# A two-layer graph network: layer 1's edge loop built on 128-wide one-hots and node-major sums, node blocks worked outside the loops

## The chip, the cores and the metric

One core of one Trainium2 chip runs the whole program in one launch. The metric is device time in microseconds. Below, PE is TensorE, DVE is VectorE, ACT is ScalarE, POOL is GpSimd and SP is SyncE.

## What is computed

There are 6250 nodes with 128 features and 200000 edges, sorted by their target `dst`; all numbers are float32. The reference, cut down:

```python
h = relu(layernorm(x))
z = (h @ W).reshape(N, 8, 16)                      # 8 heads of 16
el, er = (z * attn_l).sum(-1), (z * attn_r).sum(-1)
e = leaky_relu(el[src] + er[dst], 0.2)
a = exp(e - segment_max(e, dst)[dst])
agg = segment_sum(z[src] * a, dst) / segment_sum(a, dst)
x = x + agg + bias                                 # layer 1
h = relu(layernorm(x)); s, v = h @ W_up_s, h @ W_up_v      # 32 scalars, 32 vectors of 3
w0, w1, w2, w3 = split(silu(silu(ef @ A1 + b1) @ A2 + b2) @ A3)
msg = [s*y0*w0, (v.y)*w3, s*y*w1, v*y0*w2]         # per edge, s and v of src
x = x + segment_sum(msg, dst) / 10 @ W_out         # layer 2
```

## The kernel before

Both layers walk over the edges in 196 groups of 1024 (`NG`, `GE`): 8 edges (`T`) for each of the 128 partitions. A loop body of four groups (`U`) is run 49 times. The rows that the edges need are gathered from a table in HBM (`z_tab` of 136 columns in layer 1, `up_tab` of 128 in layer 2) by POOL: one indirect DMA takes 128 rows, so a group costs eight of them (L401), and a layer 1568. Four slots of `rows` let POOL run ahead; it waits for the group's indices (a small DMA that SP issues) and for `rows_free`, which DVE raises once it has read a slot.

Since the edges are sorted, a group's targets lie in a window of 48 nodes (`WIN`). **Layer 1** for a group: DVE compares the targets with a row of 0 to 47 and so makes the one-hot `hot` (L743, 384 elements in each partition); PE turns it (L977), ACT copies it out, and PE multiplies it with 48 rows of `er` that SP fetched (L987), which gives each edge its target's value. DVE computes scores (L799 to L804), ACT takes the exponential (L488), DVE multiplies the rows (L809, two halves of 512 elements). PE then sums with the *messages* as the stationary operand and `hot` as the moving one, 48 columns wide (L1004), once more for the denominators (L1006), and DVE adds the result to 48 columns of `acc_a` and `den_acc` (L771, L773), which hold features in the partitions and nodes along the free axis. **Layer 2** has an edge network on PE and ACT (L1040 to L1050, L502, L504), products on DVE (L872 to L890) and sums on PE (L1083, L1085) in the same form, added at L860 and L862.

A block of 128 nodes is finished inside the loops, as soon as no later edge can reach it (a table `ready` says when). In layer 1 that is `stage_sums` on ACT, `turn_sums` on PE and `divide_block` on DVE (L753 to L763), which also takes the block's statistics for the next norm. In layer 2 it is `stage_block`, `map_block` (four matmuls with the output weights, L1062), `add_block` (L843) and a store. After a loop only the last one to three blocks are left.

Ahead of layer 1 come loads, POOL's fills (L393 to L397), the targets' conversion (L564), statistics of x in seven chunks (L546), and `node_lin` with `node_rows`, which make `z_tab`; SP stores it in seven transfers. Between the layers the accumulators are filled with zero by POOL (L422 to L424), while ACT, PE and DVE make `up_tab` (L447, L453, L929, L934, L621, L629). POOL starts layer 2's gathers once that table is stored. The order on every engine is that of the code, and nothing reorders it.

## Time and profile before

| | |
|---|---|
| time, median of 3 runs | 4219.83 us (4218.35 to 4221.5) |
| span of the profiled execution | 5708.3 us |
| first gather, last of layer 1, first and last of layer 2 (start) | 91.58, 2845.44, 2942.36, 5666.08 us |
| PE busy in that span | 3872.9 us |
| POOL busy | 3121.2 us |
| DVE busy | 1850.8 us |
| ACT busy | 547.9 us |

Of the profiled execution there is no time but its span, and the span is far longer than the runs that were timed. A row of the timeline gives the start, how long the work took, and in brackets how long the engine had stood idle and what ended that. "128*128 128x48 x2" at a matmul is the stationary tile, then the moving one; one float32 matmul of the program leaves two records. Rows of POOL are the making of an indirect DMA's descriptors, not the transfer. A row of windows gives the stretch, its length, busy us (and instructions) of PE, PE's weight loads, DVE, ACT and POOL, then the granted clock of PE as a share of full speed, the DMA engines' share and GB/s.

### The profile page before, as it was taken

The page shows a single profiled execution, that of the slowest core. Times are in us where ns is not written, and L with a number is a line of the kernel's source. Part 1 is how long each engine was busy: PE and PEld are TensorE (multiplying, and loading weights), DVE is VectorE, ACT ScalarE, POOL GpSimd, SP SyncE. Part 2 cuts the span into 40 slices and gives each one's busy share as a digit, 9 for nine tenths or more (in the row PEclk, how much of TensorE's full clock was granted, in tenths as well). Part 3 has the DMA queues.
Part 4 walks back from the last instruction along what each step waited for, and adds up shares of the span by engine and source line. Part 5 has one row for each costly group of instructions (what it writes and reads, how often), then busy time and mean ns, then how long its engine had stood idle before and what let it go on. Part 6 is the DMA issues. An engine that isn't in the chain of part 4 may idle for free.

```text
span 5708.3 us, 68375 instructions
## 1 busy us (share of the span) xinstructions
PE 3872.9 (68%) x18070; PEld 2962.4 (52%) x18071; DVE 1850.8 (32%) x4774; ACT 547.9 (10%) x1093; POOL 3121.2 (55%) x3153
## 2 busy tenths in 40 slices
PE   3566666766666666666657776776777776667767
PEld 2455555555555555555545555555555555555545
DVE  6122222222222222222234443433333434333334
ACT  1000000000000000000021111111111111111111
POOL 4555555555555555555535555555555555555554
PEclk8555555555555555555567777777777877777777
DMA  3111111111111111111111111111111111111111
GB/s 75 40 40 40 40 40 41 41 42 40 41 40 41 40 41 39 41 40 40 40 43 41 42 45 41 44 45 41 42 43 43 44 44 41 44 40 43 42 41 34
DMA packets 259081, 239.77 MB, mean 42 GB/s; under 512 B 179890, under 2 KB 205596, under 8 KB 259068
## 3 DMA queue, kind: packets, MB, share of 16 engines
q0 software_dynamic: 100352, 212.14, 15.2%
q1 hardware_dynamic: 158572, 26.68, 2.6%
q10 hardware_dynamic: 144, 0.80, 0.0%
q14 instruction: 9, 0.07, 0.0%
q8 instruction: 4, 0.07, 0.0%
HBM read 229.11 MB, written 10.23 MB: 42 GB/s over the span
## 4 chain that ended last, share of the span: by engine, by line
another core or an unknown queue 43%; PE 22%; issue 17%; DVE 11%; DVEq 4%; ACT 2%; DMA 0%; ACTq 0%; SPq 0%
PE pair L1085 5%; PE pair L1050 5%; DVE share L809 4%; PE pair L1044 3%; PE pair L1083 3%; PE pair L1040 2%; DVEq L768 2%; ACT share L502 1%; PE pair L1062 1%; PE pair L1004 1%; PE pair L987 1%; DVE share L743 1%; DVE share L800 1%; DVE share L799 1%
## 5 line engine op out<-in xcount | busy, mean ns | idle before, releaser
L401 POOL DMA_INDIRECT rows<-z_tab,idx x1568 | 1531.6, 977 | 1290.3 <-DVEq L813 748.9
L401 POOL DMA_INDIRECT rows<-up_tab,idx x1568 | 1549.4, 988 | 1208.6 <-DVEq L896 718.1
L1004 PE MATMUL pair<-share 128*128 128x48 f32 x3136 | 1000.7, 416 | 122.6 <-issue 122.3
L1004 PEld LDWEIGHTS pair<-share 128*128 128x128 f32 x3136 | 808.4, 317 | 279.4 <-issue 273.3
L1085 PE MATMUL pair<-share 128*128 128x144 f32 x3136 | 859.4, 359 | 129.8 <-issue 129.3
L1083 PEld LDWEIGHTS pair<-share 128*128 128x128 f32 x3136 | 587.2, 219 | 443.2 <-issue 342.9
L1050 PE MATMUL pair<-a_bd,share 128*128 128x256 f32 x1576 | 465.9, 448 | 394.1 <-ACT share L504 371.1
L877 DVE TENSOR_TENSOR share<-share,y_sb 128x768 f32<-128x768 f32 x392 | 375.6, 958 | 977.1 <-remote 662.1
L1083 PE MATMUL pair<-share 128*128 128x48 f32 x3136 | 585.7, 269 | 140.0 <-issue 121.2
L1085 PEld LDWEIGHTS pair<-share 128*128 128x128 f32 x3136 | 561.3, 221 | 128.6 <-issue 128.0
L987 PE MATMUL pair<-er_win,share 96*128 96x32 f32 x1576 | 377.2, 404 | 333.0 <-issue 268.4
L1050 PEld LDWEIGHTS pair<-a_bd,share 128*128 128x128 f32 x1576 | 341.7, 227 | 460.2 <-ACT share L504 381.8
L1006 PE MATMUL pair<-share 128*8 128x48 f32 x3136 | 521.0, 264 | 74.5 <-issue 73.7
L987 PEld LDWEIGHTS pair<-er_win,share 96*128 96x128 f32 x1576 | 351.2, 328 | 370.0 <-issue 368.8
L977 PE MATMUL pair<-ident,share 128*96 128x128 f32 x788 | 214.6, 428 | 367.4 <-DVE share L743 359.5
L887 DVE TENSOR_TENSOR share<-rows,pair 128x384 f32<-128x384 f32 x784 | 396.6, 548 | 10.0 <-DMA rows<-up_tab,idx 10.0
L799 DVE TENSOR_TENSOR share<-rows,pair 128x64 f32<-128x64 f32 x196 | 43.3, 221 | 1067.9 <-remote 681.7
L1044 PE MATMUL pair<-share,a_bd 128*128 128x512 f32 x396 | 283.9, 808 | 137.3 <-ACT share L502 133.6
L977 PEld LDWEIGHTS pair<-ident,share 128*96 128x96 f32 x788 | 126.5, 188 | 413.7 <-DVE share L743 386.0
L1006 PEld LDWEIGHTS pair<-share 128*8 128x8 f32 x3136 | 164.1, 91 | 242.9 <-issue 103.6
L502 ACT ACTIVATE share<-pair,vec 128x512 f32<-128x512 f32 x198 | 136.0, 687 | 1368.3 <-remote 737.8
L809 DVE TENSOR_TENSOR share<-rows,share 128x512 f32<-128x512 f32 x392 | 251.9, 683 | 0.0
(138 smaller groups left out, 2085.3 us busy)
## 6 DMA issues: line engine op xcount, KB each, us to landing
rows<-z_tab,idx POOLq DMA_INDIRECT x1568
rows<-up_tab,idx POOLq DMA_INDIRECT x1568
idx<-in_src SPq DMA_DIRECT2D x396, 4.0 KB
er_win<-er_tab SPq DMA_DIRECT2D x396, 3.0 KB
ef_sb<-in_edge_f SPq DMA_DIRECT2D x198, 32.0 KB
z_tab<-rows SPq DMA_DIRECT2D x7, 476.0 KB, 3.1
y_sb<-in_edge_y SPq DMA_DIRECT2D x198, 16.0 KB
x_sb<-in_x SPq DMA_DIRECT2D x7, 448.0 KB, 6.9
```

The source lines that it names most:

```text
L401: pool.indirect_dma_start(out=rows[:, s, t, 0:width], out_offset=None, in_=table, in_offset=bass.IndirectOffsetOnAxis(ap=indices[:, t:t + ...
L809: ins = v.tensor_tensor(msg[:, h, ts, :].rearrange("p t (h f) -> p t h f", f=PER_HEAD), rows[:, s, ts, 0:HIDDEN].rearrange("p t (h f) -> p ...
L877: v.tensor_tensor(wy[:, hf, :, :].rearrange("p t (k w) -> p t k w", k=4), bc(eq[:, hf, :, :], 2, 4), bc(y_sb[:, s, ts, :], 3, WIN), ALU.mult)
L887: v.tensor_tensor(prod[:, hf, :, half, 0:96].rearrange("p t (i u) -> p t i u", u=MUL), g_v, bc(tp[:, :, lo:lo + 32], 2, 3), ALU.mult)
L977: mm = t.transpose(bank[0][0:2 * WIN, j * P:(j + 1) * P], hot[:, s, 2 * j:2 * j + 2, :].rearrange("p t w -> p (t w)"), ident[:, :])
L987: mm = t.matmul(bank[6 + h][:, j * 32:j * 32 + 32], hotT[0:2 * WIN, h, j * P:(j + 1) * P], er_win[0:2 * WIN, s, :], start=True, stop=True)
L1004: t.matmul(bank[2 + h][:, 0:WIN], msg[:, h, i, :], hot[:, s, i, :], start=(i == 0), stop=(i == T - 1))
L1006: mm = t.matmul(bank[4 + h][0:HEADS, 0:WIN], a_sb[:, h, i, :], hot[:, s, i, :], start=(i == 0), stop=(i == T - 1))
L1044: t.matmul(bank[5], a2_bd[:, :], h1_sb, start=True, stop=True).then_inc(s_l2["h2"], 1)
L1050: mm = t.matmul(bank[2 * h + j // 2][:, (j % 2) * 256:(j % 2) * 256 + 256], h2_sb[:, h, j * P:(j + 1) * P], a3_bd[:, :], start=True, stop= ...
L1083: t.matmul(bank[6 + h][:, 0:WIN], prod[:, hf, j, 0, :], wy[:, hf, j, 0:WIN], start=st, stop=en, skip_group_check=True)
L1085: mm = t.matmul(bank[6 + h][:, WIN:4 * WIN], prod[:, hf, j, 1, :], wy[:, hf, j, WIN:4 * WIN], start=False, stop=en, skip_group_check=True)
```

## The change

Layer 1's loop is written anew, with a layout of its own over the accumulators (`lay`).

- The one-hot is 128 wide: `hot` has 1024 elements in each partition, made from `dst_col`. It is now the *stationary* operand, the messages the moving one: 136 columns, 16 features and a one for each head, so that the denominators come out of the same matmul. Sums have nodes in the partitions (`sums_all`, 98 slots of 64 nodes' step with 136 columns), and DVE adds one slot for each group.
- The turned one-hot is no longer made by PE and ACT. SP reads the group's 1024 targets into all partitions (`load_targets`), and DVE compares them with each partition's node number (`turned_hot`).
- `er` stays in SBUF (`er_slots`), together with a bound that keeps the exponent at or under zero; the score has three DVE instructions and not four.
- The indices are loaded once (`idx_all`); DVE copies eight columns for each group (`set_idx`), in layer 2 too.
- The node blocks leave both loops. Between the layers a loop of seven takes chunks of 7 blocks; at the end PE maps all 49 blocks straight from the accumulators.
- More of the targets' arithmetic stands ahead of layer 1, in `set_windows`.

The core of the diff (`divide_block`, `stage_sums`, `turn_sums`, `stage_block`, `map_block` and `add_block` are taken out):

```diff
+        SUM0 = COLS + MW
+        sums_all = lay(COLS, 1 + SLOTS1, MW)
+        sums_at = lay(SUM0, SLOTS1, MW)
+        sums_even = lay(SUM0, NB, 2, MW)
+        sums_odd = lay(COLS, NB, 2, MW)
+        AUX = SUM0 + SLOTS1 * MW
+        er_slots = lay(AUX, NB, 2, 2 * HEADS)
+        er_flat = lay(AUX, SLOTS1, 2 * HEADS)
+        dst_col = lay(AUX + 32 * NB, NG + 1, T)
+        node_id = lay(AUX + 32 * NB + (NG + 1) * T, NG + AHEAD)
+        dst_bc = lay(AUX + 32 * NB + (NG + 1) * T + NG + AHEAD, 2, GE)
...
+            def load_targets(s, group):
+                sp.dma_start(dst_bc[:, s % 2, :], dst_tab[bass.ds(group * GE, GE)].partition_broadcast(P)).then_inc(s_l1["in"][s % 2], 16)
...
-            for s_l, tab, width in ((s_l1, z_tab, ZW), (s_l2, up_tab, HIDDEN)):
-                if s_l is s_l2:
-                    pool.wait_ge(s_mid["agg_staged"], NB)
-                    pool.memset(den_acc, 0.0).then_inc(zeroed, 1)
-                    pool.memset(max_acc, 0.0).then_inc(zeroed, 1)
-                    pool.memset(acc_a[:], 0.0).then_inc(zeroed, 1)
-                    table_stored(s_mid)
...
+                            hold(pool, idx_set, (n + before) * U + (s + 1))
+                            hold(pool, freed, n * (2 * U) + (2 * s + 2))
...
+            pool.wait_ge(G["summed"], 1)
+            pool.memset(acc[:], 0.0).then_inc(zeroed, 1)
+            table_stored(s_mid)
...
+                cols = dst_col[:, 0:NG, :]
+                own.after(v.tensor_tensor(cols, dst_rel[:, :, :], bc(slot_f[:, :], 2, T), ALU.subtract))
+                turn_back = tab_sb[:, 0:BU + 4, :].rearrange("p a f -> p (a f)")[:, 0:NG * T]\
+                    .rearrange("p (g t) -> p g t", t=T)
+                own.after(v.scalar_tensor_tensor(out=turn_back, in0=cols, scalar=float(P), in1=bc(odd_f[:, :], 2, T),
+                                                 op0=ALU.is_ge, op1=ALU.mult))
+                own.after(v.tensor_tensor(cols, cols, turn_back, ALU.subtract))
+                own.after(v.tensor_tensor(dst_rel[:, :, :], dst_rel[:, :, :], bc(win_f[:, :], 2, T), ALU.subtract))
...
+            v.tensor_copy(er_slots[HALF:P, :, 1, :], er_slots[HALF:P, :, 0, :]).then_inc(G["er_ready"], 1)
+            v.tensor_copy(er_slots[0:HALF, 0:NB - 1, 1, :], er_slots[0:HALF, 1:NB, 0, :]).then_inc(G["er_ready"], 1)
+
+            def set_idx(s, group):
+                v.tensor_copy(idx[:, s, :], idx_all[:, bass.ds(group, 1), :].rearrange("p a t -> p (a t)"))\
+                    .then_inc(idx_set, 1)
...
             def one_hot(s, group):
-
                 v.tensor_tensor(hot[:, s, :, :],
-                                bc(dst_rel[:, bass.ds(group, 1), :].rearrange("p a t -> p (a t)"), 2, WIN),
-                                bc(iota[:, :], 1, T), ALU.is_equal).then_inc(s_l1["hot"], 1)
...
+                                bc(dst_col[:, bass.ds(group, 1), :].rearrange("p a t -> p (a t)"), 2, P),
+                                bc(iota[:, :], 1, T), ALU.is_equal)
...
+            def turned_hot(s, group, arrived):
+                dve.wait_ge(s_l1["in"][s % 2], arrived)
+                v.tensor_scalar(hotT[:, s % 2, :], dst_bc[:, s % 2, :], node_id[:, bass.ds(group, 1)], None,
+                                ALU.is_equal).then_inc(s_l1["turned"], 1)
...
-                        own_l1.after(v.tensor_tensor(e3[0], el_e, er_e[:, :, 0:8], ALU.add))
-                        own_l1.after(v.scalar_tensor_tensor(out=e3[1], in0=e3[0], scalar=NEG_SLOPE, in1=e3[0],
-                                                            op0=ALU.mult, op1=ALU.max))
-                        own_l1.after(v.tensor_tensor(e3[2], e3[1], er_e[:, :, 8:16], ALU.subtract))
-
-                        v.tensor_scalar(e3[3], e3[2], 0.0, None, ALU.min).then_inc(s_l1["score"], 1)
...
+                        own_l1.mark(v.tensor_tensor(e_sb[:, h, :, 0, :], el_e, er_e[:, :, 0, :], ALU.add))
+                        own_l1.after(v.scalar_tensor_tensor(out=e_sb[:, h, :, 1, :], in0=el_e, scalar=NEG_SLOPE,
+                                                            in1=er_e[:, :, 1, :], op0=ALU.mult, op1=ALU.add))
+                        v.tensor_tensor(e2_sb[:, h, :, :], e_sb[:, h, :, 0, :], e_sb[:, h, :, 1, :], ALU.max)\
+                            .then_inc(s_l1["score"], 1)
+                        set_idx(s, q * U + (s + U))
+                        turned_hot(s, q * U + (s + AHEAD), k * IN1 + q * 32 + (16 * (s // 2) + 32))
                         one_hot((s + 1) % U, q * U + (s + 1))
...
-                            ins = v.tensor_tensor(msg[:, h, ts, :].rearrange("p t (h f) -> p t h f", f=PER_HEAD),
-                                                  rows[:, s, ts, 0:HIDDEN].rearrange("p t (h f) -> p t h f", f=PER_HEAD),
-                                                  bc(a_sb[:, h, ts, :], 3, PER_HEAD), ALU.mult).then_inc(s_l1["msg"], 1)
-                        dve.wait_ge(s_l1["msg"], (n * U + (s + 1)) * 2)
-                        dve.sem_inc(s_l1["rows_free"], 1)
+                            v.scalar_tensor_tensor(
+                                out=msg[:, h, ts, :].rearrange("p t (h f) -> p t h f", f=RW),
+                                in0=bc(a_sb[:, h, ts, :], 3, RW), scalar=1.0,
+                                in1=rows[:, s, ts, 0:MW].rearrange("p t (h f) -> p t h f", f=RW),
+                                op0=ALU.min, op1=ALU.mult).then_inc(s_l1["msg"], 1)
...
+                own_sum.mark(v.tensor_tensor(even[HALF:P], even[HALF:P], odd[HALF:P], ALU.add))
+                own_sum.after(v.tensor_tensor(even[0:HALF], even[0:HALF], before[0:HALF], ALU.add), hold)
+                cells = even.rearrange("p k (h f) -> p k h f", f=RW)
+                own_sum.after(v.tensor_scalar(rden, cells[:, :, :, PER_HEAD:RW].rearrange("p k h a -> p k (h a)"), TINY,
+                                              None, ALU.max), hold)
+                own_sum.after(v.reciprocal(rden, rden), hold)
+                own_sum.after(v.tensor_tensor(part_rows.rearrange("p k (h f) -> p k h f", f=PER_HEAD),
+                                              cells[:, :, :, 0:PER_HEAD], bc(rden, 3, PER_HEAD), ALU.mult), hold)
+                own_sum.after(v.tensor_tensor(x_sb[:, bs, :], x_sb[:, bs, :], part_rows, ALU.add), hold)
+                own_sum.mark(v.memset(rden, 0.0))
+                norm_stats(q)
...
-                for j in range(HT):
-                    mm = t.matmul(bank[6 + h][:, j * 32:j * 32 + 32], hotT[0:2 * WIN, h, j * P:(j + 1) * P],
-                                  er_win[0:2 * WIN, s, :], start=True, stop=True)
+                at = pe.value_load(slot_i[0:1, bass.ds(group + 1, 1)], min_val=0, max_val=SLOTS1 - 1)
+                pe.wait_ge(s_l1["turned"], count + (AHEAD + 1))
+                for i in range(T):
+                    mm = t.matmul(bank[6 + h][:, i * 16:i * 16 + 16], hotT[:, h, i * P:(i + 1) * P],
+                                  er_flat[:, bass.ds(at, 1), :].rearrange("p a f -> p (a f)"), start=True, stop=True)
                 mm.then_inc(s_l1["er"], 1)
 
-            with pe.Fori(0, passes) as k:
-                turn(0, k * (NG + 1))
...
-                            t.matmul(bank[2 + h][:, 0:WIN], msg[:, h, i, :], hot[:, s, i, :],
-                                     start=(i == 0), stop=(i == T - 1))
-                            mm = t.matmul(bank[4 + h][0:HEADS, 0:WIN], a_sb[:, h, i, :], hot[:, s, i, :],
+                                pe.wait_ge(s_l1["msg"], n * (2 * U) + (2 * U + 2 * s + i // HT + 1))
+                            if i == 0:
+                                pe.wait_ge(s_l1["added"], n * U + (s + 1))
+                            mm = t.matmul(bank[2 + h][:, 0:MW], hot[:, s, i, :], msg[:, h, i, :],
                                           start=(i == 0), stop=(i == T - 1))
...
+            pe.wait_ge(s_l2["added"], passes * NG + 1)
+            for c in range(BI):
+                for hf, (lo, hi) in enumerate(HALVES):
+                    m = 2 * c + hf
+                    if m >= 4:
+                        pe.wait_ge(s_out["added"], m - 3)
+                    for b in range(lo, hi):
+                        nodes = slice((c * BU + b) * P, (c * BU + b) * P + P)
+                        for i in range(4):
+                            mm = t.matmul(bank[m % 4][:, (b - lo) * P:(b - lo) * P + P],
+                                          acc_a[:, nodes] if i == 0 else acc_b[:, i - 1, nodes],
+                                          wo_a[:, :] if i == 0 else wo_b[:, i - 1, :], start=(i == 0), stop=(i == 3))
+                    mm.then_inc(s_out["agg"], 1)
```

DVE in layer 1's loop, one group (`acc<-acc` are `hotT` and `hot`, which lie in `acc` now; `share` holds the scores, `a_sb` and `msg`). Before:

```order
L799 TENSOR_TENSOR share<-rows,pair 128x64
...
L800 SCALAR_TENSOR_TENSOR share<-share 128x64
...
L802 TENSOR_TENSOR share<-share,pair 128x64
...
L804 TENSOR_SCALAR share<-share 128x64
...
L743 TENSOR_TENSOR share<-dst_rel,iota 128x384
...
L809 TENSOR_TENSOR share<-rows,share 128x512 x2
...
L771 TENSOR_TENSOR acc_a<-acc_a,pair 128x48
...
L773 TENSOR_TENSOR acc_b<-acc_b,pair 8x48
```

The same place in the changed kernel:

```order
L783 TENSOR_TENSOR share<-rows,pair 128x8x8
L784 SCALAR_TENSOR_TENSOR share<-rows,pair 128x8x8
...
L786 TENSOR_TENSOR share<-share 128x64
...
L726 COPY idx<-idx_all 128x8
...
L745 TENSOR_SCALAR acc<-acc 128x1024
...
L739 TENSOR_TENSOR acc<-acc,iota 128x1024
...
L794 SCALAR_TENSOR_TENSOR share<-share,rows 128x544 x2
...
L754 TENSOR_TENSOR acc<-acc,pair 128x136
```

The copy of indices and the comparison of 1024 elements are new, the one-hot has 1024 elements for 384, and the message's two halves have 544 elements for 512 in another form of instruction.

DVE between the layers, one of seven passes of the new loop (`acc<-acc` are the sums of two slots brought together; seven BN_STATS, of which one is shown, follow, then seven BN_AGGR):

```order
L822 TENSOR_TENSOR acc<-acc 64x7x136
...
L823 TENSOR_TENSOR acc<-acc 64x7x136
...
L825 TENSOR_SCALAR share<-acc 128x56
...
L827 RECIPROCAL share<-share 128x56
...
L828 TENSOR_TENSOR share<-acc,share 128x896
...
L830 TENSOR_TENSOR x_sb<-x_sb,share 128x896
...
L831 MEMSET share 128x56
L515 BN_STATS share<-x_sb 128x6
```

None of this stood behind layer 1's loop before; there `divide_block` was left for the last blocks alone.

## Rows read from the trace of the kernel before

**Rows 1.** Top of the page, and the POOL groups of its section 5 (mean ns; idle before).
```profile
span 5708.3 us, 68375 instructions
...
L401 POOL DMA_INDIRECT rows<-z_tab,idx x1568 | 1531.6, 977 | 1290.3 <-DVEq L813 748.9
L401 POOL DMA_INDIRECT rows<-up_tab,idx x1568 | 1549.4, 988 | 1208.6 <-DVEq L896 718.1
```

**Rows 2.** Timeline of PE in layer 1: start us, duration us, work [idle before <-releaser].
```profile
1520.11 0.24 PE L1004 MATMUL pair<-share 128*128 128x48 f32 x1 [1.86 <-issue]
```

**Rows 3.** Timeline of POOL, from several stretches of the span.
```profile
91.58 1.31 POOL L401 DMA_INDIRECT rows<-z_tab,idx  x1 [67.02 <-issue]
93.19 6.76 POOL L401 DMA_INDIRECT rows<-z_tab,idx  x1 [0.30 <-issue]
...
109.01 0.94 POOL L401 DMA_INDIRECT rows<-z_tab,idx  x1 [0.30 <-issue]
...
2831.72 0.94 POOL L401 DMA_INDIRECT rows<-z_tab,idx  x1 [0.30 <-issue]
...
2845.44 0.94 POOL L401 DMA_INDIRECT rows<-z_tab,idx  x1 [0.30 <-issue]
...
2942.36 0.95 POOL L401 DMA_INDIRECT rows<-up_tab,idx  x1 [33.27 <-issue]
...
5666.08 0.94 POOL L401 DMA_INDIRECT rows<-up_tab,idx  x1 [0.30 <-issue]
```

**Rows 4.** Windows of all engines, one without gathers in layer 1, one at the start.
```profile
2855.00:2890.00 35.00, 33.62 (x159) 26.20 (x158) 10.44 (x36) 3.05 (x8) 0.00 (x0) 0.50 0.01 1
...
0.00:10.00 10.00, 0.00 (x0) 0.01 (x1) 4.55 (x5) 1.29 (x2) 9.48 (x12) 1.00 0.90 242
```

**Rows 5.** Timeline of VectorE and POOL side by side.
```profile
92.45 6.68 DVE L714 TENSOR_TENSOR x_sb<-x_sb,bias_bc 128x6272 f32<-128x6272 f32 x1
...
111.97 0.22 DVE L799 TENSOR_TENSOR share<-rows,pair 128x64 f32<-128x64 f32 x1 [4.08 <-DMA rows<-z_tab,idx]
...
1504.77 0.55 DVE L743 TENSOR_TENSOR share<-dst_rel,iota 128x384 f32<-128x384 f32 x1
...
1505.23 1.28 DVE L809 TENSOR_TENSOR share<-rows,share 128x512 f32<-128x512 f32 x2
...
1505.87 1.47 POOL L401 DMA_INDIRECT rows<-z_tab,idx  x1 [0.30 <-issue]
```

**Rows 6.** Timeline of the start: VectorE's first cast, POOL's fill, statistics of one chunk.
```profile
2.07 16.09 POOL L395 MEMSET acc_b<- 128x19200 f32 x1
...
5.71 18.65 DVE L564 CAST dst_rel<-share 128x1568 f32<-128x1568 int32 x1 [4.66 <-DMA share<-in_dst]
...
32.28 1.45 DVE L546 BATCH_NORM_STATS2 share<-x_sb 128x6 f32 x7 [0.28 <-issue]
```

**Rows 7.** Timeline between the layers.
```profile
2877.31 0.22 DVE L799 TENSOR_TENSOR share<-rows,pair 128x64 f32<-128x64 f32 x1 [3.62 <-PE pair L987]
...
2889.91 0.18 DVE L773 TENSOR_TENSOR acc_b<-acc_b,pair 8x48 f32 x1
...
2890.58 0.98 DVE L739 TENSOR_SCALAR dst_rel<-dst_rel 128x1568 f32<-128x1568 f32 x1
...
2894.87 8.85 DVE L763 COPY share<-share 128x2 f32 x1 [0.16 <-DVE share L762]
...
2909.46 0.34 ACT L447 ACTIVATE share<-share,flags 128x49 f32<-128x49 f32 x1 [15.31 <-DVEq L605]
```

**Rows 8.** Timeline of the end of layer 2.
```profile
5676.19 0.83 PE L1062 MATMUL pair<-wo_b,share 128*128 128x128 f32 x6
...
5689.26 1.01 DVE L887 TENSOR_TENSOR share<-rows,pair 128x384 f32<-128x384 f32 x2
...
5700.65 1.39 PE L1062 MATMUL pair<-wo_b,share 128*128 128x128 f32 x6
...
5705.48 0.33 SPq L385 DMA_DIRECT2D out<-x_sb  x1
```

More of the change, by code:

```diff
@@ L713, in _ @@
+            for s in range(U):
+                set_idx(s, s)
             dve.wait_ge(loads["bias"], 16)
             own.after(v.tensor_tensor(x_sb[:, :, :], x_sb[:, :, :], bc(bias_bc[:, :], 1, NB), ALU.add))
-            own.after(v.tensor_reduce(least, wide[0:1, 0:NG].rearrange("p (q s) -> p q s", s=U), AX.X, ALU.min))
-            shift = 1
-            while shift < GI:
-                own.after(v.tensor_tensor(least[:, 0:GI - shift], least[:, 0:GI - shift], least[:, shift:GI],
-                                          ALU.min))
-                shift *= 2
@@ L724, in _ @@
-            own.after(v.tensor_scalar(ends, iota[0:1, 0:NB - 1], float(P), float(P), ALU.mult, ALU.add))
-            own.after(v.tensor_tensor(past, bc(least, 2, NB - 1), bc(ends, 1, GI), ALU.is_ge))
-            own.after(v.tensor_reduce(least, past, AX.X, ALU.add))
-            v.memset(ready[:, 0:2], 0)
-            v.tensor_copy(ready[:, 2:GI + 2], least).then_inc(G["ready_set"], 1)
-            dve.wait_ge(G["ready_set"], 1)
-            dve.wait_ge(G["er_stored"], 32)
+            dve.wait_ge(G["lin_stored"], 16)
@@ L738, in next_pass @@
                 own_pass.after(v.tensor_copy(win_i[0:1, 1:NG + 1], win_f[0:1, :]))
-                own_pass.after(v.tensor_scalar(dst_rel[:, 0:NG, :], dst_rel[:, 0:NG, :], -float(WIN), None, ALU.add))
-            def one_hot(s, group):
-                v.tensor_tensor(hot[:, s, :, :],
-                                bc(dst_rel[:, bass.ds(group, 1), :].rearrange("p a t -> p (a t)"), 2, WIN),
-                                bc(iota[:, :], 1, T), ALU.is_equal).then_inc(s_l1["hot"], 1)
-            own_block = Own(dve, sem("own_block"))
@@ L846, in _ @@
-            dve.wait_ge(zeroed, 13)
+                own_pass.after(v.tensor_scalar(dst_rel[:, :, :], dst_rel[:, :, :], -float(WIN), None, ALU.add))
+            dve.wait_ge(zeroed, 14)
             dve.sem_inc(s_l2["added"], 1)
```

556 lines of the change are left out of this document (258 added, 298 removed).

## The prediction

> **What bounds the kernel now.** I read the page first. Its span, 5708.3 us [rows 1], is 1488 us longer than the median of the timed runs, 4219.8 us, so nothing may be read off the span before it is known what is in it. The timeline shows it: PE crawls through stretches in which it waits for nothing that the profile names, as in [rows 2], while the engines behind it stand too. So busy shares say little here; I look for an engine that does not stand.
>
> That is POOL. Where POOL is not held up, eleven gathers take 2845.44 - 2831.72 = 13.72 us, 1.247 us each: 0.944 of work and 0.303 between two [rows 3]. There are 3136 of them, 3911 us. The means of 977 and 988 ns [rows 1] add 0.033 x 1568 = 51 and 0.044 x 1568 = 69 us, 120 together, some 8 of it at the first gathers. Around that lie three stretches in which POOL makes no gather. The first gather starts at 91.6 us [rows 3]. Between the layers: about 2.0 us for rows to land (the eighth gather of the first group ends at 109.95, L799 starts at 111.97 [rows 3, 5]), 12.6 from L799 of the last group to its last sum at 2889.9 [rows 7], and 52.5 from there to the next gather at 2942.4 [rows 3, 7], 67 us. At the end: about 1.7 us to land (an estimate beside those 2.0), then 19.0 from L887 of the last group to the span's end [rows 8, 1], 21 us. The sum is 3911 + 120 + 92 + 67 + 21 = 4211 us, and the median is 4219.8. **The timed runs are POOL's gathers, one after another**, 10.3 us for a group, and everything else hides behind them but those three stretches. PE alone does not explain it: with no gather about, it is busy 33.6 of 35 us [rows 4] and takes 9.3 us for a group at clock 0.50, 11 where a block is in it, 9.7 in the mean.
>
> So the change leaves 3911 us where they are: the same 3136 gathers (the wider rows cost nothing that the rows show, 136 columns against 128 have the same 0.94). What it can move is the four other terms. What PE, ACT and SP save in the loop falls into their idle time.
>
> **What a gather waits for.** A gather that starts at 1505.87 takes 1.47 us, not 0.94; it ends 0.83 us after L809's second half does, at 1506.51 [rows 5]. The second gather of all takes 6.76 us and ends 0.82 us after L714 [rows 3, 5]. So a gather needs something at about 0.12 us into its work, and a DVE instruction that reads two operands from SBUF keeps it away until it ends. The Trainium skill, SBUF — State Buffer, Who interferes with whom, has DVE and GpSimd share a port pair, taken whole: by copies and tensor_scalar in their double-rate modes, and for reads by anything with two SBUF inputs; but it infers that a tensor_tensor does not stall descriptor making. The trace disagrees with that inference, by the 0.53 us above. By the inference layer 1's term below would come from the new tensor_scalar alone, 0 to 0.4 us a group; by the rows it comes from all four long instructions.
>
> **Layer 1's loop, +98 us.** I lay DVE's new sequence against POOL's pace. Lengths: tensor_tensor 0.55 for 384 elements and 6.68 for 6272 [rows 5] give 0.15 + 1.04 ns an element, so the 128-wide one-hot takes 1.23 us (0.55 before) and a message half 0.72 (0.68). The comparison L745 takes 0.76, if it runs at the rate of L739, 0.98 us for 1568 [rows 7] and 0.07 for its operand from memory (an estimate), and 1.3 if it does not. DVE starts when a group's rows land, 2.0 us after its eighth gather, which is 0.45 us into the second gather of the next group. With the steps of before (0.25 from one dependent instruction to the next), L745 lies at 0.60 to 1.36 after landing, the one-hot to 2.49, the messages at 2.40 to 3.12 and 3.04 to 3.76. The third gather wants in at 0.92, waits to 1.36 (+0.44), and the fourth wants in at 2.61 and waits to 3.12 (+0.51). That is 0.95 us a group; over other landing times the same exercise gives 0.6 to 1.1, and I take 0.85. Before, the same layout gives 0.05 to 0.54; the means of the page say 0.22 and the long gather of [rows 5] 0.53 in a steady group; I take 0.35. The difference, 0.50 x 196 = 98 us, has bounds of -0.1 (the new form of the message does not count) and +0.95 (L745 at the slow rate): -20 to +186.
>
> **Ahead of layer 1, +8 us.** L564 takes 18.65 us where 1 would do: it starts when POOL's fills of 19200 and 6400 columns are over [rows 6]. The fills shrink to 13464 + 1568 + 198 columns, 12.8 us at 16.09/19200, so it ends about 6 us earlier; a second cast costs 1.0. `set_windows` gets three passes over 1568 elements more, 1.79 us each by the line above, and some ten small ones of 0.3 to 0.4: +9.3, two flags +0.4. Then the first gather waits for `set_idx`, which stands behind four instructions of 0.57 us and two copies, +3.5. The `ready` table's work goes, which held gathers up for about 2 us. -6 + 1 + 9.7 + 0.7 (wider `node_lin`) + 3.5 - 2 is 7 to 8; bounds 4 and 14.
>
> **Between the layers, +44 us.** From landing to the last sum: `targets_er` and then eight matmuls stand on PE, about 10 us for 12.6, and `next_pass1` takes 2. Then the new loop runs alone: per pass two tensor_tensor of 952 elements (1.15 each), two of 896 (1.09 each), 0.7 for the reciprocal and the maximum, about 1.2 in five waits for the instruction before, 0.3 of registers, and 2.55 for statistics (one chunk as in [rows 6], start to start), 9.0 us, and 63 for seven. Before, 19.6 us lay between the last sum and L447 [rows 7], 11 of them because copies stood behind POOL's fills (8.85 in one [rows 7]). From L447 to the gather nothing changes, 32.9 us; POOL's fill of 25600 columns, 21.5 us, fits in there, and would cost up to 21.5 if it did not. After: 2 + 10 + 2 + 63.5 + 32.9 = 111, less 67: +44, bounds 36 and 60.
>
> **The end, +50 us.** Before, all but the last blocks of layer 2 were mapped in the loop at no cost, since PE had room. Now 49 blocks of four matmuls stand behind the last sum. Six records take 0.83 us at full clock and 1.39 at half [rows 8], so a block of eight takes about 1.0 and 1.75, steps included: 48 us or 86. PE is busy without a break there, so I take 52. DVE's additions, 0.7 us for four blocks, run beside it; the last one and the last store add 4.5 (before, 2.8 from the last store's issue to the end [rows 8, 1]). 1.7 + 9.5 + 0.3 + 52 + 4.5 + 3 for cold code = 71, less 21: +50, bounds 43 and 90.
>
> **Layer 2's loop** loses the index DMA and the blocks, which no gather waited for, and gets a copy of eight columns: 0, with +-20 us for gathers that meet DVE at other moments.
>
> Sum: 98 + 8 + 44 + 50 = +200 us, against 4219.8: **4420 us**. I let the 9 us that my sum lacks stand on both sides.
>
> **Rivals.**
> - *The message's new form leaves gathers alone* (14%). For it: none of the long rows is this form. Against: it reads two SBUF operands like L809. Layer 1 then gives -20 to +40, in all 4320.
> - *L745 at the slow rate, or a landing time at the bad phase* (10%): +186 in layer 1, 4510.
> - *A new bound in layer 1* (7%): SP now brings 512 KB a group into all partitions, and PE has 16 loads of 128 columns. Against: 590 KB of rows and these in 10.8 us are 102 GB/s, and the engines moved 242 GB/s at the start [rows 4]; PE needs about 9.5 us at half clock, as now. If it fails, each 1 us beyond 10.8 costs 196 us: 4500 and more.
> - *Faster: the loop of before holds its gathers up more than I think, and the new one not at all* (4%). If nearly all of the 120 us lay in layer 1 and the new loop's instructions fell between the gathers, the saving would be 120, and the three stretches at their low ends cost 83: 4183. It decides only if the new loop holds gathers up for less than 37/196 = 0.19 us a group; DVE now has 3.7 us a group of instructions that could, of a gather's 1.25 us beat.
> - The likeliest case, 65%, has its own range, 4360 to 4500.
>
> **How the numbers follow.** Range 4300 to 4510: it takes in the first rival and the likeliest case up to the slow clock at the end. 0.2% (about 8 us) is what a measurement can tell from no change. Faster 3%, within 0.2% 1%, slower 96%.
>
> **What would show it.** Right: first gather near 100 us; unheld gathers 1.25 us apart; two gathers of 1.2 to 1.5 us in a group of layer 1, each ending 0.82 us after a DVE instruction, and a mean near 1.05 us; about 63 us of DVE alone between the layers; some 50 us of L1068 at the end. PE's busy time in layer 1 will fall, and the profile's span may well fall with it, with no meaning for the timed runs. Wrong: gathers closer together than 1.247 us, a POOL that waits for `idx_set` or `msg`, or a median under 4300.

## The result, and the profile after

The changed kernel takes **4396.97 us** (median of 4 runs, 4395.53 to 4399.83) against 4219.09 of the kernel before on the same chip: ratio 1.0422, 95% interval 1.0407 to 1.0437. 4420 was forecast, with 4300 to 4510.

That holds for chips on which the kernel before takes about 4220 us. The experiments met others where its medians are 5711 to 5765 us and its 21 timed runs took 5679 to 5776; there the sign turns, as a section below shows. In the text "quick" and "slow" chip stand for these two.

Top of the page of the changed kernel, the first row of its section 4, and the POOL groups of its section 5 (mean ns; idle before):

```profile
span 4394.7 us, 55209 instructions
...
POOL 69%; issue 23%; DVE 3%; PE 2%; DMA 1%; POOLq 1%; SPq 1%; DVEq 0%; ACT 0%; ACTq 0%
...
L396 POOL DMA_INDIRECT rows<-z_tab,idx x1568 | 1636.7, 1044 | 562.7 <-issue 477.5
L396 POOL DMA_INDIRECT rows<-up_tab,idx x1568 | 1532.7, 978 | 488.3 <-issue 481.6
```

They answer to [rows 1]. Here the span and the timed runs agree, and the chain of waits is POOL's. The pause between two gathers is 0.305 us everywhere: within a loop POOL never waits for anything. But layer 1's gathers have become longer, 1044 ns against 977.

Timeline of the changed kernel, POOL, DVE and SP, from several stretches (answers to [rows 3, 5, 7]):

```profile
101.53 6.63 POOL L396 DMA_INDIRECT rows<-z_tab,idx  x1 [85.16 <-DVE idx L726]
...
1249.86 0.75 DVE L745 TENSOR_SCALAR acc<-acc 128x1024 f32<-128x1024 f32 x1
1250.33 1.09 POOL L396 DMA_INDIRECT rows<-z_tab,idx  x1 [0.30 <-issue]
1250.52 1.22 DVE L739 TENSOR_TENSOR acc<-acc,iota 128x1024 f32<-128x1024 f32 x1
1250.85 11.07 SPq L338 DMA_DIRECT2D acc<-dst_tab  x2
1251.66 1.35 DVE L794 SCALAR_TENSOR_TENSOR share<-share,rows 128x544 f32<-128x544 f32 x2
1251.73 1.47 POOL L396 DMA_INDIRECT rows<-z_tab,idx  x1 [0.30 <-issue]
...
1253.50 0.94 POOL L396 DMA_INDIRECT rows<-z_tab,idx  x1 [0.30 <-issue]
...
2214.77 0.94 POOL L396 DMA_INDIRECT rows<-z_tab,idx  x1 [0.30 <-issue]
...
2291.85 21.44 POOL L433 MEMSET acc<- 128x25600 f32 x1 [76.13 <-DVEq L835]
2324.09 0.95 POOL L396 DMA_INDIRECT rows<-up_tab,idx  x1 [10.80 <-issue]
...
3005.67 0.41 DVE L894 TENSOR_TENSOR share<-rows,pair 128x256 f32<-128x256 f32 x1
3005.74 0.94 POOL L396 DMA_INDIRECT rows<-up_tab,idx  x1 [0.30 <-issue]
...
3006.39 0.96 DVE L882 TENSOR_TENSOR share<-share,y_sb 128x768 f32<-128x768 f32 x1
3006.99 1.17 POOL L396 DMA_INDIRECT rows<-up_tab,idx  x1 [0.30 <-issue]
...
4333.40 0.94 POOL L396 DMA_INDIRECT rows<-up_tab,idx  x1 [0.30 <-issue]
```

In a group of layer 1 two gathers are held. The one at 1250.33 ends at 1251.42, 0.81 us after the turned one-hot L745; the one at 1251.73 ends at 1253.20, 0.82 after the first message half (1251.66 + 0.72). The next, with nothing long beside it, takes 0.94. Laid gather by gather against DVE's rows, 194 gathers that meet L794 are 0.521 us longer than 0.944 in the mean, 196 that meet L745 0.249; L739 is met by 2. Together that is 0.770 us a group. (A gather "meets" the instruction that is at work 0.12 us after the gather's start.)

Layer 2 of the same kernel shows both kinds side by side. L882 reads two operands from SBUF, and the gather at 3006.99 ends 0.81 us after it; 249 gathers that meet it are 0.181 us longer in the mean. L891 and L894 read one operand from PSUM ("pair" in the names is PSUM), and the gather at 3005.74, under L894, takes 0.94; the 172 that meet L891 and the 64 that meet L894 alone lose 0.01 us at most.

Windows of the changed kernel: layer 1, the new middle, layer 2, the new end.

```profile
110.00:2200.00 2090.00, 1404.03 (x6216) 1350.00 (x6215) 791.86 (x1746) 111.26 (x242) 1616.73 (x1554) 0.59 0.37 104
2216.00:2292.00 76.00, 7.40 (x32) 7.09 (x32) 57.24 (x168) 1.62 (x3) 0.15 (x1) 0.52 0.01 1
...
2330.00:4330.00 2000.00, 1773.73 (x8569) 1373.93 (x8569) 1075.14 (x2532) 268.66 (x391) 1524.61 (x1561) 0.83 0.22 56
4346.00:4392.00 46.00, 43.49 (x390) 43.30 (x388) 9.56 (x15) 0.00 (x0) 0.00 (x0) 1.00 0.23 67
```

In layer 1 PE has 7.3 us of work a group and idles for the rest of 10.8; in the middle DVE works nearly alone for 76 us; at the end PE maps blocks for 46 us at granted clock 1.00, its upper level of 2.4 GHz.

### The profile page after: what moved, and what is told of

It reads as the page before. It is cut to its first block, busy times and chain, and to the rows that moved or that the text cites. A ratio compares the mean times of both kernels' runs of the same rounds, so it can differ in the third digit from the quotient of the medians.

```text
span 4394.7 us, 55209 instructions
## 1 busy us (share of the span) xinstructions
PE 3310.9 (75%) x15640; PEld 2840.8 (65%) x15641; DVE 2047.1 (47%) x4758; ACT 430.6 (10%) x748; POOL 3206.6 (73%) x3154
## 3 DMA queue, kind: packets, MB, share of 16 engines
q0 software_dynamic: 100352, 218.57, 19.5%
## 4 chain that ended last, share of the span: by engine, by line
POOL 69%; issue 23%; DVE 3%; PE 2%; DMA 1%; POOLq 1%; SPq 1%; DVEq 0%; ACT 0%; ACTq 0%
POOL rows L396 69%; PE pair L1068 1%; DMA rows<-up_tab,idx 1%; PE pair L940 1%; DVE share L891 1%; POOLq L249 0%; POOLq L419 0%; SPq L271 0%; POOLq L250 0%; DVE share L894 0%; DMA win_dram<-share 0%; DVE share L592 0%; DVE acc L823 0%; DVE x_sb L830 0%; DVE share L828 0%
## 5 line engine op out<-in xcount | busy, mean ns | idle before, releaser
L396 POOL DMA_INDIRECT rows<-z_tab,idx x1568 | 1636.7, 1044 | 562.7 <-issue 477.5
L976 PE MATMUL pair<-acc 128*128 x3168 | 697.2, 370 | 709.7 <-DVE acc L745 709.7
L976 PEld LDWEIGHTS pair<-acc 128*128 128x128 f32 x3168 | 677.0, 325 | 764.5 <-issue 764.5
L1045 PEld LDWEIGHTS pair<-share 128*128 128x128 f32 x3136 | 627.8, 234 | 532.0 <-DVE share L894 401.1
L1047 PE MATMUL pair<-share 128*128 128x144 f32 x3136 | 885.5, 373 | 0.0
L1045 PE MATMUL pair<-share 128*128 128x48 f32 x3136 | 611.0, 282 | 226.0 <-DVE share L894 226.0
L996 PE MATMUL pair<-share,acc 128*128 128x136 f32 x3136 | 759.3, 435 | 0.0
L996 PEld LDWEIGHTS pair<-share,acc 128*128 128x128 f32 x3136 | 716.5, 332 | 0.0
L891 DVE TENSOR_TENSOR share<-rows,pair 128x384 f32<-128x384 f32 x784 | 398.0, 549 | 678.8 <-DMA rows<-up_tab,idx 667.3
L1047 PEld LDWEIGHTS pair<-share 128*128 128x128 f32 x3136 | 585.7, 233 | 0.0
L882 DVE TENSOR_TENSOR share<-share,y_sb 128x768 f32<-128x768 f32 x392 | 375.5, 958 | 111.9 <-PE pair L1047 101.7
L1018 PE MATMUL pair<-share,a_bd 128*128 128x512 f32 x396 | 295.5, 839 | 1.6 <-ACT share L483 1.6
L794 DVE SCALAR_TENSOR_TENSOR share<-share,rows 128x544 f32<-128x544 f32 x392 | 265.4, 719 | 0.0
L739 DVE TENSOR_TENSOR acc<-acc,iota 128x1024 f32<-128x1024 f32 x197 | 240.0, 1218 | 0.0
L485 ACT ACTIVATE share<-pair,vec 128x512 f32<-128x512 f32 x198 | 136.1, 687 | 940.9 <-PE pair L1018 940.9
L1014 PE MATMUL pair<-ef_sb,a_bd 16*128 16x512 f32 x396 | 223.7, 645 | 4.6 <-DMA ef_sb<-in_edge_f 4.6
L483 ACT ACTIVATE share<-pair,vec 128x512 f32<-128x512 f32 x198 | 136.0, 687 | 813.3 <-PE pair L1014 813.3
```

Of the source, the lines that this page charges most:

```text
L396: pool.indirect_dma_start(out=rows[:, s, t, 0:width], out_offset=None, in_=table, in_offset=bass.IndirectOffsetOnAxis(ap=indices[:, t:t + ...
L739: v.tensor_tensor(hot[:, s, :, :], bc(dst_col[:, bass.ds(group, 1), :].rearrange("p a t -> p (a t)"), 2, P), bc(iota[:, :], 1, T), ALU.is_ ...
L794: v.scalar_tensor_tensor(out=msg[:, h, ts, :].rearrange("p t (h f) -> p t h f", f=RW), in0=bc(a_sb[:, h, ts, :], 3, RW), scalar=1.0, in1=r ...
L882: v.tensor_tensor(wy[:, hf, :, :].rearrange("p t (k w) -> p t k w", k=4), bc(eq[:, hf, :, :], 2, 4), bc(y_sb[:, s, ts, :], 3, WIN), ALU.mult)
L891: v.tensor_tensor(prod[:, hf, :, half, 0:96].rearrange("p t (i u) -> p t i u", u=MUL), g_v, bc(tp[:, :, lo:lo + 32], 2, 3), ALU.mult)
L976: mm = t.matmul(bank[6 + h][:, i * 16:i * 16 + 16], hotT[:, h, i * P:(i + 1) * P], er_flat[:, bass.ds(at, 1), :].rearrange("p a f -> p (a ...
```

## What was tried where POOL sets the time

Four kernels were measured side by side on a quick chip (the kernel before: 4222.60 us, 12 runs).

**after2**, the changed kernel unedited. 

> The changed kernel once more, unedited, beside the kernel before, because the four experiments so far ran on a chip where the kernel before took 5765 us and PE stood in stretches. Theory: the chip, or what else runs beside the job, sets whether PE stands; the change's +4.2% holds only where it does not. If the kernel before takes about 4219 us here: 4397 us, ratio 1.042. If the kernel before takes about 5760 us: the change has fewer PE instructions and came out at 0.975 with one operand moved to PSUM, so it should be near 5650 us, ratio 0.98. Rival: what moved a_msg to 0.975 was the operand alone; then a ratio of 1.04 here too.

Measured: 4404.67 us, ratio 1.0427 (1.0410 to 1.0444).

**a_l1_2**, the change with one operand of each long DVE instruction of layer 1 in PSUM:

```diff
-                                bc(iota[:, :], 1, T), ALU.is_equal)
+                                bc(iota_ps, 1, T), ALU.is_equal)
...
-                v.tensor_scalar(hotT[:, s % 2, :], dst_bc[:, s % 2, :], node_id[:, bass.ds(group, 1)], None,
-                                ALU.is_equal).then_inc(s_l1["turned"], 1)
+                v.tensor_tensor(hotT[:, s % 2, :], dst_bc[:, s % 2, :],
+                                nid_ps[:, bass.ds(group, 1)].broadcast_to([P, GE]), ALU.is_equal).then_inc(s_l1["turned"], 1)
...
-                                in0=bc(a_sb[:, h, ts, :], 3, RW), scalar=1.0,
+                                in0=bc(a_ps[h][:, ts, :], 3, RW), scalar=1.0,
```

> The change with one operand of each long DVE instruction of layer 1 (one-hot, turned one-hot, message) read from PSUM. Theory (a gather waits for the end of a DVE instruction that has SBUF on both reads, or runs at a double rate): the time that gathers are held in layer 1 falls from 0.770 to under 0.05 us a group, 0.74 x 196 = 145 us less than the change where PE does not stand: 4252 us if the kernel before takes 4219. Rival (the held time comes from something else of the group, such as the 512 KB broadcast): no gain, 4397. Where the kernel before takes about 5760 us: POOL's gathers are short, and the time is set by PE's stops; about 5690 as before.

Measured: 4251.75 us (ratio 1.0069, 1.0053 to 1.0086), **152.9 us less than after2**, 145 expected. The timeline of a_l1_2, POOL and DVE in one group:

```profile
1249.12 1.22 DVE L748 TENSOR_TENSOR acc<-acc,pair 128x1024 f32<-128x1024 f32 x1
1249.51 0.95 POOL L399 DMA_INDIRECT rows<-z_tab,idx  x1 [0.30 <-issue]
1250.26 1.22 DVE L742 TENSOR_TENSOR acc<-acc,pair 128x1024 f32<-128x1024 f32 x1
...
1250.76 0.94 POOL L399 DMA_INDIRECT rows<-z_tab,idx  x1 [0.30 <-issue]
1251.39 1.35 DVE L801 SCALAR_TENSOR_TENSOR share<-pair,rows 128x544 f32<-128x544 f32 x2
1252.01 0.95 POOL L399 DMA_INDIRECT rows<-z_tab,idx  x1 [0.30 <-issue]
```

DVE is busy for longer than before (the turned one-hot takes 1.22 us instead of 0.75), and no gather notices: of 587 that meet one of the three, none is over 0.01 us longer than 0.944. So it is not DVE's activity, its length or the 512 KB broadcast (still there) that holds a gather, but an instruction with SBUF on both reads, or the tensor_scalar (this run changes both at once). The Trainium skill, SBUF — State Buffer, Who interferes with whom, says the first part, that an instruction "with at most one SBUF input, outside the 2-port perf modes, does not contend with GpSimd", and the trace agrees; its inference that a tensor_tensor leaves descriptor making alone stays contradicted, by [rows 5] and by the tensor_tensor L882 above; the 0.52 us at L794 are another form of instruction, with the same two SBUF operands.

**b_l1_2**, the kernel before with the same done to its one-hot and its message (ACT writes the exponential twice; not shown: the row of 0 to 47 in PSUM, and the denominators' sums moved into the numerators' bank to make room for it):

```diff
+                        nc.scalar.activation(a_ps[h].rearrange("p t h -> p (t h)"), e_sb[:, 3, :], ACT.Exp)\
...
-                                                  bc(a_sb[:, h, ts, :], 3, PER_HEAD), ALU.mult).then_inc(s_l1["msg"], 1)
+                                                  bc(a_ps[h][:, ts, :], 3, PER_HEAD), ALU.mult).then_inc(s_l1["msg"], 1)
```

> The kernel before with one operand of the one-hot and of the message read from PSUM, the exponential written twice. Theory: the gathers' wait in layer 1, about 0.31 us a group, goes: 61 us less, 4158 us if the kernel before takes 4219. Rival (those waits are hidden in a slack that POOL has): 4219. Where the kernel before takes about 5760 us: no gain, about 5985 as before.

Measured: **4175.53 us, ratio 0.9886 (0.9869 to 0.9902)**, the fastest of all: 47.1 us less, 61 expected. So the kernel before holds its gathers in layer 1 for 47.1/196 = 0.24 us a group. Timeline of POOL in b_l1_2, from four stretches:

```profile
91.65 1.33 POOL L403 DMA_INDIRECT rows<-z_tab,idx  x1 [67.09 <-issue]
...
2056.02 0.94 POOL L403 DMA_INDIRECT rows<-z_tab,idx  x1 [0.30 <-issue]
...
2122.54 0.95 POOL L403 DMA_INDIRECT rows<-up_tab,idx  x1 [32.93 <-issue]
...
4151.27 0.94 POOL L403 DMA_INDIRECT rows<-up_tab,idx  x1 [0.31 <-issue]
```

Its span is 4174.9. With these rows the terms of the kernel before, whose own trace comes from a slow chip, can be put down one by one (below).

**a_both**, a_l1_2 with layer 2's blocks back in its loop, as the kernel before has them:

```diff
+                            if s == 1 and hf == 0:
+                                blocks(dve, q + 1, add_block)
...
+                        if s == 1:
+                            mapped = blocks(pe, q + 1, map_block)
...
+            last_blocks(pe, map_block)
```

> The change with the operands in PSUM and with layer 2's node blocks put back into its loop. Theory: the first takes 145 us, the second the tail from 60 to about 25, 35 us: 4397 - 180 = 4217 us, no better than the kernel before at 4219, since head (+8) and middle (+41) stay. Rival (layer 2's blocks in the loop hold gathers up or delay PE): 4240 and more. Where the kernel before takes about 5760 us: near 5550, by the 5509 of the blocks alone.

Measured: 4234.65 us (ratio 1.0026, 1.0016 to 1.0037), 17 us less than a_l1_2 and not 35. POOL's first and last gather of layer 2 in a_both:

```profile
2176.60 1.44 POOL L427 DMA_INDIRECT rows<-up_tab,idx  x1 [11.81 <-issue]
...
4209.33 0.94 POOL L427 DMA_INDIRECT rows<-up_tab,idx  x1 [0.30 <-issue]
```

The end shrinks as expected, from 60.6 us in a_l1_2 (4186.34 to 4246.92) to 22.5 (4210.27 to its span of 4232.8), -38. But layer 2's gathers now take 2033.7 us from first to last and not 2011.6: **22 us of the 38 are given back**, because gathers meet DVE at a worse moment (mean 992 ns, 978 in a_l1_2). They do not meet the product of two SBUF operands more often (252 times at L950, 260 at the same instruction, L889, of a_l1_2), but earlier in its work, and are held 0.282 us in the mean and not 0.181. The blocks in the kernel before were not free either.

## What was tried on the slow chips

Some of these kernels had first run on a slow chip (the kernel before: 5764.89 us, 7 runs). a_msg is the change with only the message's operand moved, a_blk2 the change with only layer 2's blocks back in its loop.

> The changed kernel, but ACT writes the exponentials into PSUM, so that the message instruction reads one operand from SBUF (the rows) and one from PSUM. Nothing else moves. Theory (the timed runs are POOL's gathers one after another, and a gather is held up by a DVE instruction that reads two operands from SBUF or runs at double rate): the fourth gather of each layer-1 group, held up by the message for 0.52 us in the changed kernel's trace, falls back to 0.94 us, the third stays near 1.2; 196 x 0.52 = 102 us less, 4295 us. Rival A (the new form of instruction does not matter, the hold-up comes from how long DVE is busy or from a copy): no change, 4397. Rival B (layer 1 is set by the chain from DVE to PE): no change either, and POOL's pace not tighter.

> The one before, and also the row of 0 to 127 for the one-hot and the node numbers for the comparison in PSUM; the comparison becomes a tensor_tensor at single rate, so DVE works 0.46 us a group longer than in the changed kernel. Theory: hardly a gather of layer 1 is held up any more, 0.77 us a group fall to under 0.05; about 145 us less than the changed kernel, 4252 us. Rival (DVE's own time or its chain counts): not faster than the one before, perhaps slower by up to 90 us.

> The kernel before, with the row of 0 to 47 and a second copy of the exponentials in PSUM, and the denominators' sums moved into the numerators' bank to make room; ACT does one more small instruction a group. Layer 2 and all three stretches without gathers are as before. Theory: layer 1's gathers are no longer held up by L743 and L809. How much that was in the timed runs of before could only be bounded, 0.05 to 0.54 us a group; with layer 2 at the changed kernel's 2010 us, what remains for layer 1 is 0.31 us a group, so about 60 us less, 4159 us (4115 to 4210). Rival (before, layer 1 is set by PE at 9.7 us a group and more, not by gathers): no change, 4219.

> The changed kernel, with layer 2's node blocks back in the loop as they were before (the ready table, stage, map and add of a block, a store for each). Theory: the stretch after the last gather falls from 60.4 to about 21 us, and the loop has room for the blocks; the ready table costs about 2 us at the start: 37 us less, 4360 us. Rival (PE or DVE have no room in layer 2's loop): the loop grows by up to 49 x 1.7 = 83 us and the kernel gets slower by 45.

Later came a_msg once more with two cut kernels, in which six of the eight gathers of each group are made, so that the edges of the other two are left out of the sums, while PE does all its products as before (the kernel before: 5710.73), and last the changed kernel alone (the kernel before: 5712.41).

```diff
-                for t in range(T):
+                for t in range(TG):
                     pool.indirect...
```

> The change with the message's one operand in PSUM, the turned one-hot and the one-hot left as they are. Theory: the message holds the fourth gather of each group for 0.52 us, the turned one-hot (a tensor_scalar) the third for 0.25, so this takes away 0.52 x 196 = 102 us less whatever a freed POOL then meets: 4397 - 102 = 4295 us where the kernel before takes 4219, with the third gather still held by 0.25. Rival (all is one effect of the group, and a gather let through here is caught elsewhere): over 4350. Where the kernel before takes about 5760 us: near 5614 as before.

> The kernel before with six of the eight gathers of each group, in both layers; the rows of the last two of each slot are zeros, so a quarter of the sums is left out. It asks what lies behind the gathers. Theory: gathers take 6 x 1.247 = 7.5 us a group, and PE with 9.7 at half clock becomes the bound of layer 1: 196 x 9.7 = 1900 us there; layer 2, where PE takes 1201.5 of 1350 us at clock 0.86, stays near 1800 us; with 180 for head, middle and end about 3880. Rival (gathers alone count): 3136 x 0.75 x 1.247 + 300 = 3230 us.

> The same for the changed kernel: six of the eight gathers of each group, a quarter of the sums left out. Theory: PE is busy 1404 us of 2090 in layer 1, 7.2 us a group, so the gathers with their holds, 7.5 + 0.77 = 8.3 us, still set it: 1620 us there, against 1900 of the kernel before in the same cut; layer 2 as there, 1800; head, middle and end 270: about 3690, so faster than b_six by 190. Rival (DVE or the transfers of layer 1 are a bound of their own): layer 1 stays near 2000 and the time near 4050.

> The changed kernel unedited, once more, for the case that was not met yet: the kernel before at about 5710 to 5765 us. Theory: there PE's stops set the time, the change has 13% fewer PE instructions, and a_msg came out at 0.975 and 0.964 of the kernel before; the one operand that a_msg moves is worth at most 0.52 x 196 = 102 us, so the change itself is at 0.97 to 0.99 there, that is faster than the kernel before. Rival: the order of the two kernels is the same whatever PE does, ratio 1.04. If the kernel before takes about 4219 us here, the ratio of 1.042 comes back and the question stays open.

| kernel | us | ratio to before, 95% |
|---|---|---|
| after3 | 5437.16 | 0.9505 (0.9440 to 0.9570) |
| a_blk2 | 5508.70 | 0.9569 (0.9526 to 0.9613) |
| a_msg_2, a_msg | 5490.78, 5613.74 | 0.9638 (0.9580 to 0.9695), 0.9751 (0.9708 to 0.9793) |
| a_l1 | 5692.28 | 0.9897 (0.9854 to 0.9941) |
| b_l1 | 5985.27 | 1.0388 (1.0344 to 1.0432) |
| a_six | 4384.41 | 0.7685 (0.7652 to 0.7719) |
| b_six | 4560.21 | 0.7969 (0.7920 to 0.8018) |

All expectations that counted on POOL failed here, and the order is turned over: **the change is faster than the kernel before by 5%** (0.97 to 0.99 was expected), and the edits that move operands to PSUM make both kernels slower. They do shorten the gathers here too: the mean in layer 1 is 949 ns in a_l1 and 1016 in after3. Whether the shorter gathers cost the time or something else about the PSUM operands, no run separates. The blocks of layer 2 in the loop make no difference that can be told: the intervals of a_blk2 and after3 meet. a_msg_2, expected near 5614, came out at 5491 on another slow chip.

The waits of PE show one difference. In layer 1 of after2, the quick chip (engine, line, what it waited for: us in all, times, longest):

```profile
PE pair L976 <- DVE acc L745: 701.4, 195, 16.4
```

and in after3, the same program on a slow one:

```profile
PE pair L976 <- issue: 668.4, 471, 4.3
PE pair L996 <- issue: 395.9, 316, 3.1
PE pair L976 <- DVE acc L745: 124.7, 54, 16.3
```

On the quick chip PE waits once for each group, for its data. On the slow one it stops 787 times for 1064 us, 1.35 us each, with nothing named that it waits for. Timeline of PE in after3 there:

```profile
1254.21 0.19 PE L976 MATMUL pair<-acc 128*128 x1 [1.25 <-issue]
1255.63 0.19 PE L976 MATMUL pair<-acc 128*128 x1 [1.23 <-issue]
1257.73 0.19 PE L976 MATMUL pair<-acc 128*128 x1 [1.91 <-issue]
...
1260.57 0.19 PE L976 MATMUL pair<-acc 128*128 x1 [1.23 <-issue]
1261.26 0.19 PE L976 MATMUL pair<-acc 128*128 x1 [0.50 <-issue]
```

The starts stand 0.70, 1.41 or 2.10 us apart, where after2 has them 0.23 apart on average in its busy stretches (6209 records in 1404 us of work). It is the picture of [rows 2]; by that and by its span, 5708.3 us, the kernel before was profiled on such a chip.

These stops come while gathers are made. In after3 between the layers (2540 to 2640) and once layer 2's gathers are over (from 5331) no row of PE's waits says "issue", and the kernel before worked 33.6 of 35 us in such a stretch [rows 4]. With a quarter of the gathers away the stops shrink by more than that quarter: in the waits of a_six

```profile
PE pair L978 <- issue: 464.2, 427, 4.4
...
PE pair L998 <- issue: 148.1, 179, 2.4
```

612 us against the 1081 of after3 over its whole span on the same two lines. The cut kernels take 1150 us (b_six) and 1053 us (a_six, against after3, measured at another time) less, more than the 784 x 1.249 = 979 us of the gathers that they leave out. That a_six is 176 us below b_six, 190 expected, says that behind the gathers the new layer 1 has less work, as its 7.3 us of PE a group do; the absolute times expected there (3690, 3880) were for a quick chip and were not met.

But these stops do not set the time. In after3 layer 2, first gather to last, takes 2684 us against the 2010 of the quick chip, a loss twice that of layer 1 (2426 against 2114), and there all stops of PE with "issue" come to 48 us. And over the whole span the profile of the kernel before has 515 of them for 753 us, b_l1, the slowest, 207 for 327, and the faster changed kernel 829 for 1129. Fewer matmul records (18070 before, 15640 after) do not mean fewer stops either.

What the slow chip's traces show in both layers is that other engines learn late that PE is done. Timeline of after3 in layer 2, without weight loads ("remote": the profile finds no instruction that raised the flag just then):

```profile
4001.38 1.02 PE L1018 MATMUL pair<-share,a_bd 128*128 128x512 f32 x2
...
4003.80 0.48 PE L1047 MATMUL pair<-share 128*128 128x144 f32 x2
...
4005.00 0.69 ACT L485 ACTIVATE share<-pair,vec 128x512 f32<-128x512 f32 x1 [4.81 <-remote]
...
4007.67 1.12 PE L1014 MATMUL pair<-ef_sb,a_bd 16*128 16x512 f32 x2
...
4013.94 0.94 POOL L396 DMA_INDIRECT rows<-up_tab,idx  x1 [0.30 <-issue]
4017.84 0.69 ACT L483 ACTIVATE share<-pair,vec 128x512 f32<-128x512 f32 x1 [12.14 <-remote]
4017.88 0.20 DVE L865 TENSOR_TENSOR acc<-acc,pair 128x48 f32 x1 [18.39 <-remote]
...
4024.92 0.94 POOL L396 DMA_INDIRECT rows<-up_tab,idx  x1 [10.03 <-DVE idx L726]
```

ACT's L485 waits for L1018, which ended 2.6 us before; L483 for L1014, 9.0 us before; DVE's L865 for the sums of L1047, 13.6 us before. Then DVE is late with everything, POOL has no indices and stands for 10 us. Laid pair by pair over all of layer 1, DVE's sum L754 starts 7.1 us in the mean after the later of PE's last product (L996) and its own last work, and up to 41.2 us; 65 of 196 are over 3 us late, and in 64 of its waits the flag (semaphore) that came in last, by the profile, is that of L996, over 1.5 us after the product's end. In after and after2 no such start is over 0.26 us late. On every slow chip the longest delay before this sum is 16 to 42 us; on the quick ones none is over 3 us. POOL's idle time between gathers, beyond 0.31 us each, adds up to 1128 us in after3 and 109 in after2, and the spans differ by 1015; in b_l1 and b_l1_2 it is 1866 and 65, and the spans differ by 1816. So the slow chip's time is POOL standing behind engines that were released late.

The kernel before has one such hand-over more in each group of layer 1: ACT copies out what PE turned. On the quick chip (b_l1_2) that copy starts 1.3 us after PE has turned it in the mean, in the profile of before 4.7, in b_l1 7.9. The change has taken this step away. It also leaves PE time in each group (busy 1404 of 2090 us), where in b_l1_2 PE is busy 1837 of 1950 us of layer 1. Either would explain why the change loses less there; no run tests it. Nor does any say what delays the flags, whether it is the gathers' traffic, or why one chip does it and another does not. All this stays open.

## Why the prediction was right, and where it was not

Each term, from the rows above; "before" is b_l1_2 plus the 47.1 us in layer 1's loop:

| term | forecast | before | after | measured |
|---|---|---|---|---|
| head: first gather | +8 | 91.65 | 101.53 | +9.9 |
| layer 1's loop, first gather to end of last | +98 | 1965.3 + 47.1 | 2114.2 | +101.8 |
| between the layers | +44 | 65.6 | 108.4 | +42.8 |
| layer 2's loop | 0 | 2029.7 | 2010.2 | -19.5 |
| end | +50 | 22.7 | 60.4 | +37.7 |
| sum | +200 | | | +172.7 |

The two columns come from traces taken at different times; measured side by side, the kernels differ by 177.9 and 182.1 us. Of the 27 us that the forecast has too much, 12 are the end and 19.5 layer 2. The layer 2 of the kernel before is taken to be that of b_l1_2, which differs from it only in layer 1.

- **What bounds the kernel** (gathers at 1.247 us, one after another, and three stretches without any): right, on a quick chip. Its own sum, 4211, was 9 off; head 92, middle 67 and end 21 are now 91.7, 65.6 and 22.7.
- **What a gather waits for**: right, and now shown by a_l1_2 and b_l1_2. Of the change, 0.85 us a group was forecast and 0.770 measured; of the kernel before 0.35 against 0.24. Both were too high, and their difference, 0.50 against 0.53, was not; that the two errors cancelled is luck. In the layout the fourth gather was to wait 0.51, which is 0.521; the third 0.44, which is 0.25, since L745 starts 0.35 us before that gather in the mean and not 0.20, and so is done sooner. The rival that the message's new form leaves gathers alone is refuted by those 0.521 us.
- **Head and middle**: right within 2 us, though my items add up to 6.9 us for the head, not 8, and in the middle to 9.2 us a pass, not 9.0, and 110.4 us in all, not 111. The seven passes take 8.8 us each. The first gather waits for the copy of L726, and POOL's fill of 21.44 us fits under the making of `up_tab`.
- **The end**: +50 was forecast, +38 measured. The term that was mis-sized is the time of a block, 1.0 to 1.75 us with 52 us for all 49 of them taken: blocks follow each other by 0.89 us at granted clock 1.00, about 44 us. The 3 us of the sum for cold code are shown by no run: PE stands 0.72 us until DVE's last sum lets the first block begin, at 4345.45, 11.1 us after the last gather, where the sum had 14.5.
- **Layer 2, "no gather waited for the blocks"**: this step was wrong. a_both shows the blocks in the loop at 22 us, and so their removal gives back about what the table's -19.5 says. The prediction looked for gathers that wait for the blocks' flags, and left +-20 for gathers that meet DVE at other moments; it was that.
- **The span of 5708 us**: here the reading failed. I wrote that nothing may be read off the span, and that a shorter span after the change would have no meaning for the timed runs. On slow chips the timed runs of the kernel before take just that, and the change is 5% faster there. The forecast came out because the given times were those of a quick chip. The second case needed a sum of its own, over the flags that PE raises and the others wait for. [rows 1] has its sign: POOL's idle time there, 1290 and 1209 us, ends mostly with a flag of DVE, which does not fit a kernel that is bound by its gathers.

## What to carry to other kernels

Where a chain of indirect DMAs sets the time, look at what DVE runs beside it: one operand of each long instruction in PSUM (and a tensor_scalar written as a tensor_tensor) took 153 us off the change and 47 off the kernel before, though it made DVE busier. It did so on a quick chip; on a slow one the same edits made the programs slower by some 4%. Before work is moved out of a loop, or into it, count it at the gathers too and not only at the end that it shortens. When a profile's span is far from the timed runs, take both as real and work the change out for each.

## What the runs showed of the hardware

- A gather of 128 rows takes 0.944 us and the next follows 0.305 later, in every kernel here; held, it ends 0.81 to 0.83 us after the DVE instruction that held it does. What holds it is an instruction with two SBUF operands (L794, L882) or the tensor_scalar L745. A DVE instruction of 1.22 us with one operand in PSUM costs it at most 0.01.
- The same program takes 4397 us on one chip and 5437 on another, 4219 and 5765 the kernel before, within 1.3% over the runs of a chip. On the slow chips PE starts its matmuls 0.7, 1.4 or 2.1 us apart in places while gathers run, and not when none do, and other engines start up to 41 us after the PE product that they wait for.
- There, moving the operands to PSUM makes the program slower, though its gathers are shorter: b_l1 by 3.9%, and the change by 4.7% of its time from after3 to a_l1 (measured at two times, at which the kernel before differs by 0.9%).
